# Reordering the end of a quantised stage, weighting rows earlier, and cutting two loads into paced pieces

## The chip, the cores and the metric

The kernel runs on one core of a Trainium2 chip. The metric is the time of one execution in device microseconds (us), lower is better. The engines are PE (matmul), PEld (its weight loads), DVE (vector), ACT (scalar), POOL (GpSimd) and SP (which here issues DMAs only). Each runs its own instruction list in order, and semaphores tie the lists together.

## The reference, cut to what matters

```
x = x + tanh(g_xattn[0]) * state_space(ctx, layernorm(x))
x = x + tanh(g_ffn[0])   * quantised_ffn(layernorm(x))      # 256 -> 1024 -> 256, rows rounded to 8 bits
x = x + tanh(g_xattn[1]) * attention_16_heads(layernorm(x), ctx)
x = x + tanh(g_ffn[1])   * moe_16_experts_top4(layernorm(x)) + shared, sigmoid gate
x = x + tanh(g_xattn[2]) * map_2(layernorm(x), ctx)          # softmax(Q K^T) of ctx alone, applied to x
x = x + tanh(g_ffn[2])   * ffn_with_hadamard(layernorm(x))
x = x + tanh(g_xattn[3]) * map_3(layernorm(x), ctx)
x = x + tanh(g_ffn[3])   * moe_8_experts_top2(layernorm(x)) + shared
```

x is 4 x 256 tokens by 256 columns, ctx is 4 x 256 by 128. In the quantised stage each row of the hidden product is scaled by its largest magnitude / 127, rounded, clipped and multiplied by the down matrix. A routed stage is `silu(x Wg) * (x Wu)`, times the token's weight for the expert, times `Wd`, summed over experts.

## The kernel before, in words

The 1024 tokens lie in 8 tiles of 128 rows and in two halves of 4 tiles. x stays in SBUF. Four parts follow one another: `M` (state space), `F0` (quantised stage), `A1` (attention) and `F` (three feed-forward stages, with the two maps beside them). All f32 products but those of F0 are made of three fp32r matmuls (`mm3`, lines L418 to L420) from a high and a low part of each operand; ACT copies the high part (L852) and DVE or POOL subtracts the low one.

**F0** goes by tiles t = 0 to 7. PE: `gate_up(t)` (L529), `down(t - 3)` (L541), the transposes of the rounded hidden rows `hidden_T(t - 2)` (L554); ACT: Silu (L1023), rounding (L1049), copy of the transposed rows; DVE: product (L1495), the row's largest magnitude (L1498 to L1501), `within_8_bits` (L1483), `output` (L1475). Beside it the inputs of the second half are normalised and quantised (`stats`, `row_scales`, `quantise_x`, `quantised`), and near its end the first four key units of the attention are made in four banks (`key_unit`; their squares by ACT L1042, sums by DVE L1531 `first_key_norms`, roots by POOL L1860) and the first half's rows are normalised (`stats(0)`, POOL's root L1828, `normalise(0)` L1287) and transposed (L413). The last tile's steps are handed to A1 as closures.

**A1** makes 32 passes i (16 heads by two halves). A pass is: queries and the next keys, scores (12 matmuls), their maximum (DVE L1652), Exp (ACT L1180), the row sum's reciprocal (DVE L1684), the weighting of the probabilities by it (POOL L1931), transposes (L732), products with the context and with the folded value-output matrix. POOL's list of a pass is norms, parts of the weights, query norms, then that weighting. The second half's rows must be normalised (`stats(1)`, `normalise(1)`), transposed and split (`x_lo(2)`, L1307) before pass 16.

**F** makes 100 steps g, each one tile of 128 hidden columns for 512 tokens: steps 0 to 55 are the first stage (28 by two halves), 56 to 71 the second, 72 to 99 the third (14 by two halves, of which all but the first two of each half are routed). PE's list at g: `gate_up(g)` (12 matmuls of 512 columns), `side(2g)`, `down(g - 2)` (12 of 256 columns), `side(2g + 1)`. `gate_up(g)` waits for `f_h_lo` of g - 2, since the product is kept in the PSUM bank of its gate. The order on ACT at g: high part of g - 1, Silu of g, side work, issue of DMAs for the routing rows of g + 2, weight parts. DVE's list at g before the change: `weighted(g - 1)` (L1779), `rows_lo(g - 1)` (L1786), `silu_up(g)` (L1579), then side work. `side` runs what the table `beside` puts at a place: normalising, routing, and the maps, which pass through PSUM bank 7 in one fixed order. The first map item is at place 12, so in step 6; it waits for the map weights (`loaded(pe, "am3k")`, L786). The mixing of the second stage's down matrix (L1760, L1768 to L1770) lies at places 22 to 75.

The routing rows of a step (`f_cw`, one expert's weights broadcast over the partitions) come by DMA from ACT's queue (L1082). All weight loads come from SP's queue in the order of `LOADS`; those of step 3 start when A1 has ended:

```python
("f1b", f1b, 3, "f1b"), ("am2q", ...), ("am2k", ...), ("f2w", f2w, 3, "f2"), ("am3q", ...), ("am3k", ...)
```

Of the kernel before, what the change touches and what calls it, by code (L numbers as in the profile page):

```python
# [14 lines left out]
def flamingo_kernel(nc, dram, out):  # L15
# [155 lines left out]
    ktok = [place("B1a", f"a_k_tok{i}", [P, TH, 4, P]) for i in range(2)]  # L171
    ctkh = place("B1a", "a_ctx_tok_hi", [P, NT, P], f32r)
    PTl = place("B1a", "a_PT_lo", [P, 2, HALF], f32r)
    voh, vol = ([place("B1a", f"a_wvo_{n}{i}", [P, DM], f32r) for i in range(2)] for n in ("hi", "lo"))
# [45 lines left out]
    def S(name):  # L220
        if name not in sems:
# [14 lines left out]
        ("f1b", f1b, 3, "f1b"), ("am2q", aw[0], 3, "map"), ("am2k", aw[1], 3, "map"), ("f2w", f2w, 3, "f2"),  # L236
        ("am3q", aw[2], 3, "map"), ("am3k", aw[3], 3, "map"),
# [3 lines left out]
                  for name, _, step, group in LOADS}  # L241

# [91 lines left out]
    put_norm(3, 1, P4 + 17, P4 + 19, P4 + 20, P4 + 22, P4 + 23, P4 + 24, P4 + 26, P5, P5 + 1)  # L334
# [35 lines left out]
    def _(sp):  # L370
        reached = 0

# [5 lines left out]
        for name, dst, step, group in LOADS:  # L378
            if step > reached:
# [13 lines left out]
                reached = step  # L393
            full = tuple(slice(None) for _ in dst.shape)
# [10 lines left out]
    def _(pe):  # L405
# [108 lines left out]
        def ffn0(k, m_output):  # L514
# [44 lines left out]
            for t in range(NT + 2):  # L559
                if t == 3:  # L560
                    pe.wait_ge(S("m_res"), 2)
                    quantised_inputs(1)
                if t < NT:
                    gate_up(t)
# [65 lines left out]
        def attn1(k, ffn0_rest):  # L630
# [50 lines left out]

            keys_queries(0)
            last_hidden_T()
            keys_T(0)
            query_sums(0)
            last_down()
            for i in range(HEADS2 + 2):
                if i + 1 < HEADS2:
                    keys_queries(i + 1)
                if i >= 2:  # L690
# [10 lines left out]
                if i == 1:  # L701
                    pe.wait_ge(S("q_out"), NT)
                    transpose_norm(1, ("A1", 1), (0, 1))
                if i < HEADS2:
                    pe.wait_ge(S("a_kT"), i + 1)
                    pe.wait_ge(S("a_ql"), i + 1)
                    if i:
                        pe.wait_ge(S("a_exp"), i)
                    for t in range(TH):
                        sl = slice(t * P, (t + 1) * P)  # L710
                        kv = slice((t // 2) * DM, (t // 2 + 1) * DM)
                        last = mm3(ps[:, 2 + t // 2, (t % 2) * DM:(t % 2 + 1) * DM], qh[i % 2][:, sl], ql[i % 2][:, sl],
                                   kh[:, kv], kl[:, kv], True, True)
# [1342 lines left out]
```

## Time and profile before

| | us |
|---|---|
| median of 3 runs | 1051.15 (1043.31 to 1052.46) |
| the profiled execution | 1049.61 |
| its span, first to last instruction | 1047.2 |
| PE busy | 922.8 (88%) |
| DVE busy | 728.0 (70%) |
| ACT busy | 643.8 (61%) |
| POOL busy | 484.4 (46%) |

The mean granted clock of TensorE is 0.944 of full speed. By the span's own time, F0 goes from about 180 to 235 us, A1 from there to about 540, F from there to the end. A share of the span is an average over these stages; what an engine does in one stretch is read from the stretch's own rows.

### The profile page before, as it was taken

Reading aid. Unit: us, or ns where it says so; the run is one execution under the profiler, and the core shown is the slowest. Engines: PE = TensorE matmul, PEld = TensorE weight load, DVE = VectorE, ACT = ScalarE, POOL = GpSimd, SP = SyncE. Lnnn points to the kernel's source line nnn. Section 1 sums busy time; section 2 is a strip of 40 time slices with the busy share of each in tenths; the row PEclk is TensorE's granted clock in tenths of the full one; section 3 lists DMA queues with packets and bytes.
Section 4 is the critical chain, followed back from the end, with each engine's and each line's share of the span. In section 5 each row is a group of like instructions: output and inputs, shape, how many; then the busy total and the mean of one; then the engine's idle time right before and its main releaser. Section 6 shows DMA issues by size and latency. Waiting matters only on the chain.

```text
span 1047.2 us, 15667 instructions
## 1 busy us (share of the span) xinstructions
PE 922.8 (88%) x5322; PEld 755.6 (72%) x5322; DVE 728.0 (70%) x1301; ACT 643.8 (61%) x1251; POOL 484.4 (46%) x480
## 2 busy tenths in 40 slices
PE   5277677568999999999887999889999999999998
PEld 1033233247899999999876787777888888888887
DVE  6799998885677767776654466777666565567544
ACT  5857764664777777777554565654667645454553
POOL 0266562143666666666442334345344544344342
PEclk8589989687999999999999899999999999999999
DMA  9200100003000000000039111111111410021121
GB/s 315 117 0 1 60 1 0 1 0 153 1 1 2 2 1 2 1 2 2 1 118 364 44 60 52 41 61 51 49 53 58 156 81 1 1 72 51 51 64 48
DMA packets 16602, 55.97 MB, mean 53 GB/s; under 512 B 2961, under 2 KB 4089, under 8 KB 15149
## 3 DMA queue, kind: packets, MB, share of 16 engines
q1 hardware_dynamic: 4333, 34.01, 8.5%
q10 hardware_dynamic: 12192, 20.98, 6.5%
q8 instruction: 43, 0.70, 0.3%
q14 instruction: 34, 0.28, 0.1%
HBM read 53.82 MB, written 1.16 MB: 52 GB/s over the span
## 4 chain that ended last, share of the span: by engine, by line
PE 44%; DVE 16%; issue 8%; POOL 7%; DMA 4%; ACT 3%; ACTq 1%; SPq 0%; DVEq 0%; POOLq 0%
PE psum L418 12%; PE psum L420 12%; PE psum L419 12%; POOL a_P L1931 3%; DMA am_wk<-in_am3k 3%; DVE a_max L1652 2%; POOL a_rk L1860 2%; DVE psum L1579 2%; POOL a_rq L1868 2%; DVE psum L1779 2%; PE psum L806 1%; PE psum L732 1%; PE psum L670 1%; ACTq L1082 1%; ACT f_h_hi L852 1%
## 5 line engine op out<-in xcount | busy, mean ns | idle before, releaser
L418 PE MATMUL psum<-x_norm_T_hi,f_wgu_hi 128*128 128x512 f32 x400 | 161.8, 405 | 13.8 <-DVE f_h_lo L1786 12.9
L420 PE MATMUL psum<-x_norm_T_hi,f_wgu_lo 128*128 128x512 f32 x400 | 157.9, 395 | 0.0
L419 PE MATMUL psum<-x_norm_T_lo,f_wgu_hi 128*128 128x512 f32 x400 | 157.2, 393 | 0.0
L418 PE MATMUL psum<-f_wd_hi,f_h_hi 128*128 128x256 f32 x400 | 122.7, 307 | 0.1
L1786 DVE TENSOR_TENSOR f_h_lo<-psum,f_h_hi 128x512 fp32r<-128x512 f32 x100 | 69.1, 691 | 75.7 <-ACT f_h_hi L852 75.7
L852 ACT ACTIVATE f_h_hi<-psum 128x512 fp32r<-128x512 f32 x100 | 59.2, 592 | 98.8 <-DVE psum L1779 98.5
L419 PE MATMUL psum<-f_wd_lo,f_h_hi 128*128 128x256 f32 x400 | 113.4, 284 | 0.0
L420 PE MATMUL psum<-f_wd_hi,f_h_lo 128*128 128x256 f32 x400 | 113.4, 283 | 0.0
L1579 DVE TENSOR_TENSOR psum<-f_silu,psum 128x512 f32<-128x512 f32 x100 | 69.2, 692 | 60.2 <-PE psum L420 36.6
L1952 POOL TENSOR_TENSOR m_dBu<-m_du,m_Bs 128x1024 f32<-128x1024 f32 x32 | 76.2, 2381 | 67.7 <-DVE m_du L1377 24.8
L1873 POOL TENSOR_TENSOR f_wgu_lo<-f_w,f_wgu_hi 128x512 fp32r<-128x512 f32 x44 | 56.8, 1291 | 97.3 <-ACT f_wgu_hi L852 97.3
L418 PEld LDWEIGHTS psum<-x_norm_T_hi,f_wgu_hi 128*128 128x128 f32 x400 | 76.1, 190 | 29.7 <-issue 15.3
L1873 POOL TENSOR_TENSOR f_wgu_lo<-f_wb,f_wgu_hi 128x512 fp32r<-128x512 f32 x36 | 46.6, 1295 | 106.2 <-ACT f_wgu_hi L852 106.2
L1931 POOL TENSOR_TENSOR a_P<-a_P,a_row_inv 128x1024 f32<-128x1024 f32 x32 | 60.6, 1894 | 68.6 <-DVE a_row_inv L1684 68.6
L420 PEld LDWEIGHTS psum<-x_norm_T_hi,f_wgu_lo 128*128 128x128 f32 x400 | 75.3, 188 | 17.4
L419 PEld LDWEIGHTS psum<-x_norm_T_lo,f_wgu_hi 128*128 128x128 f32 x400 | 76.2, 190 | 13.3
L419 PEld LDWEIGHTS psum<-f_wd_lo,f_h_hi 128*128 128x128 f32 x400 | 76.8, 192 | 5.0 <-issue 2.2
L418 PEld LDWEIGHTS psum<-f_wd_hi,f_h_hi 128*128 128x128 f32 x400 | 76.6, 191 | 5.2 <-issue 2.5
L420 PEld LDWEIGHTS psum<-f_wd_hi,f_h_lo 128*128 128x128 f32 x400 | 76.8, 192 | 0.0
L1088 ACT ACTIVATE f_silu<-psum 128x512 f32<-128x512 f32 x100 | 59.6, 596 | 26.1 <-PE psum L420 25.8
L852 ACT ACTIVATE a_PT_hi<-psum 128x1024 fp32r<-128x1024 f32 x32 | 32.8, 1025 | 62.9 <-PE psum L732 62.9
L1180 ACT ACTIVATE a_P<-psum,a_neg_max,a_rq 128x256 f32<-128x256 f32 x128 | 70.6, 574 | 0.8 <-DVE a_neg_max L1656 0.8
(316 smaller groups left out, 2654.7 us busy)
## 6 DMA issues: line engine op xcount, KB each, us to landing
f_cw<-r_rows ACTq DMA_DIRECT2D x38, 256.0 KB, 3.1
f_wb<-in_f1b SPq DMA_DIRECT2D x1, 6912.0 KB, 22.0
f_w<-in_f3w SPq DMA_DIRECT2D x1, 5376.0 KB, 16.7
f_wa<-in_f1a SPq DMA_DIRECT2D x1, 3840.0 KB, 11.8
w_raw<-in_w0raw SPq DMA_DIRECT2D x1, 3072.0 KB, 17.9
f_w<-in_f2w SPq DMA_DIRECT2D x1, 3072.0 KB, 31.1
f_cw<-r_rows ACTq DMA_DIRECT2D x12, 224.0 KB, 3.0
f_cw<-r_rows ACTq DMA_DIRECT2D x12, 192.0 KB, 2.8
```

What stands on the lines that cost most here:

```text
L418: mm(out, wh, xh, start=start, stop=False, **kw)
L419: mm(out, wh, xl, start=False, stop=False, **kw)
L420: return mm(out, wl, xh, start=False, stop=stop, **kw)
L852: return A(out_, in_, ACT.Copy)
L1088: A(sg[g % 2][:, :], ps[:, 2 + 2 * (g % 2), :], ACT.Silu).then_inc(S("f_sg"), 1)
L1180: last = A(Pm[i % 2][:, t, :], ps[:, 2 + t // 2, (t % 2) * DM:(t % 2 + 1) * DM], ACT.Exp, bias=nb[:, t:t + 1], scale=rq[i % 2][:, t:t + 1] ...
L1579: V.tensor_tensor(ps[:, 2 + 2 * (g % 2), :], sg[g % 2][:, :], ps[:, 3 + 2 * (g % 2), :], ALU.mult).then_inc(S("f_m"), 1)
L1652: link(V.tensor_reduce(mx[:, :], ps[:, 2:4, :].rearrange("p a (b n) -> p (a b) n", b=2), AX, ALU.max))
L1786: V.tensor_tensor(hl[g % 2][:, :], ps[:, 2 + 2 * (g % 2), :], hh[g % 2][:, :].bitcast(f32), ALU.subtract).then_inc(S("f_hl"), 1)
L1873: G.tensor_tensor(wgl[g % 2][:, :], raw_w(l, j)[:, 0:GU], wgh[g % 2][:, :].bitcast(f32), ALU.subtract).then_inc(S("f_wg"), 1)
L1931: G.tensor_tensor(Pm[i % 2][:, :, :], Pm[i % 2][:, :, :], bc(ri[:, :].unsqueeze(2), [P, TH, DM]), ALU.mult).then_inc(S("a_pn"), 1)
L1952: G.tensor_tensor(dBu[g % 2][:, :, :], du[g // NS][:, :, :], bc(Bs[g % 3][:, :].unsqueeze(1), [P, 2, HALF]), ALU.mult).then_inc(S("m_dBu"), 1)
```

## The change

**Loads.** The four map weights (64 KB each) go ahead of `f1b` (6912 KB) and `f2w` (3072 KB). These two are cut into 6 and 2 pieces, and piece n is issued when `silu_up` has been done n times (`f_m`).

**F0.** PE makes `gate_up(3)` ahead of the second half's input transposes. DVE makes the product ahead of `row_scales(1)`, and `within_8_bits` ahead of `quantise_x` and `quantised`. At t = 7 DVE makes the product, then `stats(0)`, `within_8_bits(6)`, `output(4)`, `normalise(0)`, `first_key_norms`, and only then the last tile's magnitude. The context's high and low parts are made at the end of F0. The last rounding, clipping, transposes and down product move into A1.

**A1.** The first scores come ahead of the last tile's transposes. `output(7)` and `stats(1)` come at the end of DVE's pass 0, and POOL's root for them behind the query norms of pass 0; `normalise(1)` moves from pass 0 to 1, the transposes and `x_lo(2)` from pass 1 to 2, behind the scores of the pass. A one-element Exp is put on ACT ahead of the first pass.

**F.** `weighted(g)` comes right behind `silu_up(g)`, ahead of the side work. For the last half of the third stage, the routing and its top values come half a step to one step earlier.

Buffers of A1 are placed in another order; that hunk and the ones that only rename closures are left out of the diff.

```diff
@@ -233,12 +235,15 @@
...
         ("f1r", fr[1], 2, "route"), ("f1a", f1a, 2, "f1a"),
-        ("f1b", f1b, 3, "f1b"), ("am2q", aw[0], 3, "map"), ("am2k", aw[1], 3, "map"), ("f2w", f2w, 3, "f2"),
-        ("am3q", aw[2], 3, "map"), ("am3k", aw[3], 3, "map"),
+        ("am2q", aw[0], 3, "map"), ("am2k", aw[1], 3, "map"), ("am3q", aw[2], 3, "map"), ("am3k", aw[3], 3, "map"),
+        ("f1b", f1b, 3, "f1b"), ("f2w", f2w, 3, "f2"),
         ("f3r", fr[3], 4, "route"), ("f3w", f3w, 4, "f3"),
...
                   for name, _, step, group in LOADS}
+    PIECES = {"f1b": 6, "f2w": 2}
+    for name, pieces_of in PIECES.items():
+        load_count[name] = (load_count[name][0], 16 * pieces_of)
...
@@ -331,7 +336,7 @@
...
     put_attention(3, 1, P4 + 2, P4 + 5, P4 + 7, P4 + 9, P4 + 11, P4 + 13, P4 + 15)
-    put_norm(3, 1, P4 + 17, P4 + 19, P4 + 20, P4 + 22, P4 + 23, P4 + 24, P4 + 26, P5, P5 + 1)
+    put_norm(3, 1, P4 + 17, P4 + 19, P4 + 20, P4 + 22, P4 + 23, P4 + 24, P4 + 25, P4 + 27, P5 + 1)
     put(P5 + 3, "residual", 3, 0)
...
@@ -369,6 +374,7 @@
...
         reached = 0
+        paced = 0
...
@@ -391,6 +397,13 @@
...
                 reached = step
+            if name in PIECES:
+                n = -(-dst.shape[1] // PIECES[name])
+                for a in range(0, dst.shape[1], n):
+                    paced += 1
+                    sp.wait_ge(S("f_m"), paced)
+                    sp.dma_start(dst[:, a:a + n, :], dram[name][:, a:a + n, :]).then_inc(S("ld_" + group), 16)
+                continue
             full = tuple(slice(None) for _ in dst.shape)
...
@@ -557,11 +570,11 @@
...
             for t in range(NT + 2):
+                if t < NT:
+                    gate_up(t)
                 if t == 3:
...
                     quantised_inputs(1)
-                if t < NT:
-                    gate_up(t)
                 if t == 0:
...
@@ -679,14 +692,28 @@
...
+            def scores(i):
+                pe.wait_ge(S("a_kT"), i + 1)
+                pe.wait_ge(S("a_ql"), i + 1)
+                if i:
+                    pe.wait_ge(S("a_exp"), i)
+                for t in range(TH):
+                    sl = slice(t * P, (t + 1) * P)
+                    kv = slice((t // 2) * DM, (t // 2 + 1) * DM)
+                    last = mm3(ps[:, 2 + t // 2, (t % 2) * DM:(t % 2 + 1) * DM], qh[i % 2][:, sl], ql[i % 2][:, sl],
+                               kh[:, kv], kl[:, kv], True, True)
+                last.then_inc(S("a_s"), 1)
             keys_queries(0)
-            last_hidden_T()
             keys_T(0)
             query_sums(0)
-            last_down()
+            scores(0)
             for i in range(HEADS2 + 2):
...
                     keys_queries(i + 1)
+                if i == 0:
+                    last_hidden_T()
                 if i >= 2:
...
@@ -698,20 +725,10 @@
...
                     last.then_inc(S("a_ac"), 1)
-                if i == 1:
-                    pe.wait_ge(S("q_out"), NT)
+                if 0 < i < HEADS2:
+                    scores(i)
+                if i == 2:
                     transpose_norm(1, ("A1", 1), (0, 1))
-                if i < HEADS2:
-                    pe.wait_ge(S("a_kT"), i + 1)
-                    pe.wait_ge(S("a_ql"), i + 1)
-                    if i:
-                        pe.wait_ge(S("a_exp"), i)
-                    for t in range(TH):
-                        sl = slice(t * P, (t + 1) * P)
-                        kv = slice((t // 2) * DM, (t // 2 + 1) * DM)
-                        last = mm3(ps[:, 2 + t // 2, (t % 2) * DM:(t % 2 + 1) * DM], qh[i % 2][:, sl], ql[i % 2][:, sl],
-                                   kh[:, kv], kl[:, kv], True, True)
-                    last.then_inc(S("a_s"), 1)
                 if i == HEADS2 - 2:
...
@@ -734,6 +751,8 @@
...
                     keys_T(i + 1)
+                if i == 0:
+                    last_down()
                 if i == 2:
...
@@ -1005,6 +1024,13 @@
...
+            def rounded_hidden(i):
+                act.wait_ge(S("q_inv"), i + 1)
+                if i >= 2:
+                    act.wait_ge(S("q_hq"), i - 1)
+                A(h0a[i % 2][:, :], h0[i % 2][:, :], ACT.Identity, scale=qt[i % 2][:, 2:3], bias=magic[:, :]).then_inc(S("q_r"), 1)
             def hidden_copied(t):
...
@@ -1041,17 +1067,16 @@
...
                     last.then_inc(S("a_ksq"), 1)
-                if 1 <= t <= NT:
-                    i = t - 1
-                    act.wait_ge(S("q_inv"), i + 1)
-                    if i >= 2:
-                        act.wait_ge(S("q_hq"), i - 1)
-                    A(h0a[i % 2][:, :], h0[i % 2][:, :], ACT.Identity, scale=qt[i % 2][:, 2:3], bias=magic[:, :]).then_inc(S("q_r"), 1)
+                if 1 <= t < NT:
+                    rounded_hidden(t - 1)
                 if t == 1:
...
                     hidden_copied(t - 2)
-            return lambda: hidden_copied(NT - 1)
+            loaded(act, "ctk")
+            act.wait_ge(S("q_hq"), NT - 1)
+            copy(ctkh[:, :, :], ctk[:, :, :]).then_inc(S("a_ctkh"), 1)
+            return (lambda: rounded_hidden(NT - 1)), (lambda: hidden_copied(NT - 1))
...
@@ -1133,14 +1158,17 @@
...
+            last_hidden_round, last_hidden_copy = last_hidden
             norm_T(1, (6, 5), xTh)
-            copy(ctkh[:, :, :], ctk[:, :, :]).then_inc(S("a_ctkh"), 1)
+            last_hidden_round()
             squares(0)
-            last_hidden_copy()
             keys_hi(0)
+            A(scratch[:, 21:22], epsc[:, :], ACT.Exp)
             for i in range(HEADS2 + 1):
...
                     squares(i + 1)
+                if i == 0:
+                    last_hidden_copy()
                 if i >= 2:
...
@@ -1155,7 +1183,7 @@
...
                     silu(0)
-                if i == 1:
+                if i == 2:
                     norm_T(2, (0, 1), xTa[0])
...
@@ -1486,14 +1514,21 @@
...
                     dve.wait_ge(S("q_r"), t - 1)
-                if t == 1:
-                    row_scales(1)
                 for n in range(2):
...
                                            sg0[t % 2][:, sl], ALU.mult, ALU.mult).then_inc(S("q_h"), 1)
+                if t == 1:
+                    row_scales(1)
+                if t == NT - 1:
+                    dve.wait_ge(S("q_out"), TH)
+                    stats(0)
+                    within_8_bits(NT - 2)
+                    output(NT - 4)
+                    normalise(0, xn[0])
+                    first_key_norms()
                 dve.wait_ge(S("q_h"), 2 * t + 2)
...
@@ -1505,24 +1540,16 @@
...
                     stats(1)
+                if 0 < t < NT - 1:
+                    within_8_bits(t - 1)
                 if t == 1:
...
                     quantised(1)
-                if t == NT - 1:
-                    normalise(0, xn[0])
-                if t:
-                    within_8_bits(t - 1)
-                if t >= 3:
+                if 3 <= t < NT - 1:
                     output(t - 3)
-                if t == NT - 2:
-                    dve.wait_ge(S("q_out"), TH)
-                    stats(0)
             output(NT - 3)
-            first_key_norms()
-            within_8_bits(NT - 1)
-            output(NT - 2)
-            return lambda: output(NT - 1)
+            return (lambda: within_8_bits(NT - 1)), (lambda: output(NT - 2)), (lambda: output(NT - 1))
...
@@ -1627,9 +1654,8 @@
...
             query_norms(0)
-            last_output()
-            dve.wait_ge(S("q_out"), NT)
-            stats(1)
+            for step in last_outputs[:2]:
+                step()
             for i in range(HEADS2):
...
@@ -1645,7 +1671,7 @@
...
                     V.tensor_tensor(xTl[:, c, :], ps[:, 7, :], xTh[:, c, :].bitcast(f32), ALU.subtract).then_inc(S("b7_free"), 1)
-                if i == 1:
+                if i == 2:
                     x_lo(2, (0, 1), xTa[0], xTa[1])
...
@@ -1665,6 +1691,10 @@
...
                 if i == 0:
+                    last_outputs[2]()
+                    dve.wait_ge(S("q_out"), NT)
+                    stats(1)
+                if i == 1:
                     normalise(1, xn[1])
...
@@ -1787,11 +1817,11 @@
...
                 if g:
-                    if WEIGHTED[g - 1]:
-                        weighted(g - 1)
                     rows_lo(g - 1)
...
                     silu_up(g)
+                if g < FN and WEIGHTED[g]:
+                    weighted(g)
                 if g == 1:
...
@@ -1906,12 +1936,11 @@
...
                 norms(0)
+                pool.wait_ge(S("a_ctkh"), 1)
+                G.tensor_tensor(ctkl[:, :, :], ctk[:, :, :], ctkh[:, :, :].bitcast(f32), ALU.subtract).then_inc(S("a_ctk"), 1)
                 continue
             if s == "A1":
-                pool.wait_ge(S("a_ctkh"), 1)
-                G.tensor_tensor(ctkl[:, :, :], ctk[:, :, :], ctkh[:, :, :].bitcast(f32), ALU.subtract).then_inc(S("a_ctk"), 1)
                 norm_q(0)
-                rstd_of()
                 for i in range(HEADS2 + 1):
...
@@ -1921,6 +1950,8 @@
...
                         norm_q(i + 1)
+                    if i == 0:
+                        rstd_of()
                     if i == HEADS + 5:
...
                         rstd_of()
```

## Rows read from the trace of the kernel before

**Rows 1.** Busy time by stretch, PE: stretch, length, busy (count), clock, DMA share, GB/s.

```profile
541.99:581.73 39.74, 30.14 (x154) 0.88 0.81 301
568.77:581.73 12.96, 8.82 (x26) 0.63 0.55 211
220.00:240.00 20.00, 12.30 (x58) 0.68 0.00 1
240.00:260.00 20.00, 18.13 (x91) 0.73 0.50 199
660.00:692.00 32.00, 25.92 (x147) 1.00 0.15 50
692.00:720.00 28.00, 26.22 (x146) 1.00 0.18 59
720.00:760.00 40.00, 39.81 (x219) 1.00 0.17 50
```

**Rows 2.** Who PE waited for, whole span: total us, times, longest.

```profile
PE psum L418 <- DVE f_h_lo L1786: 12.9, 11, 2.8
...
PE psum L529 <- DVE q_h L1495: 5.4, 1, 5.4
...
PE psum L786 <- DMA am_wk<-in_am3k: 4.1, 1, 4.1
...
PE psum L627 <- DVE r_weights L1574: 1.8, 1, 1.8
```

**Rows 3.** Chain of work that ended last, 540 to 580: start, us, what.

```profile
546.62 30.57 DMA am_wk<-in_am3k
```

**Rows 4.** DMA issues from 530 to 600: count, KB each, median us to landing.

```profile
f_wb<-in_f1b SPq DMA_DIRECT2D x1, 6912.0 KB, 22.0
...
f_cw<-r_rows ACTq DMA_DIRECT2D x2, 224.0 KB, 16.9
f_cw<-r_rows ACTq DMA_DIRECT2D x2, 192.0 KB, 3.2
```

**Rows 5.** Instructions in time order, DVE, first steps of F: start, us.

```profile
566.57 0.70 DVE L1779 TENSOR_TENSOR psum<-psum,f_cw 128x512 f32<-128x512 f32 x1 [4.12 <-DMA f_cw<-r_rows]
```

**Rows 6.** The same, PE: first map item and start of `gate_up(7)`.

```profile
577.32 2.05 PE L786 MATMUL psum<-ctx_T,am_wq 128*128 128x512 f32 x2 [4.14 <-DMA am_wk<-in_am3k]
...
581.73 0.56 PE L418 MATMUL psum<-x_norm_T_hi,f_wgu_hi 128*128 128x512 f32 x1
```

**Rows 7.** The same, DVE, end of F0 and passes 0 and 2 of A1.

```profile
219.24 1.41 DVE L1265 BATCH_NORM_STATS2 bn_st<-x_res 128x6 f32<-128x256 f32 x4
...
221.20 1.41 DVE L1495 SCALAR_TENSOR_TENSOR q_h<-psum,q_scales,q_sg 128x512 f32<-128x512 f32 x2
...
250.74 1.22 DVE L1652 TENSOR_REDUCE a_max<-psum 128x4 f32<-128x1024 f32 x1
...
270.33 1.22 DVE L1652 TENSOR_REDUCE a_max<-psum 128x4 f32<-128x1024 f32 x1
```

**Rows 8.** The same, ACT: squares of the key units, table load of pass 0.

```profile
223.66 2.06 ACT L1042 ACTIVATE a_P<-psum 128x512 f32<-128x512 f32 x4 [2.17 <-PE psum L420]
...
252.68 1.28 ACT L1180 ACT_TABLE_LOAD   x1
```

**Rows 9.** The same, POOL: second half's root, first weighting of probabilities.

```profile
246.20 1.01 POOL L1828 TENSOR_TENSOR rstd<-var_eps,minus_half 128x4 f32<-128x4 f32 x1 [2.82 <-DVE var_eps L1279]
...
256.56 1.89 POOL L1931 TENSOR_TENSOR a_P<-a_P,a_row_inv 128x1024 f32<-128x1024 f32 x1 [2.95 <-DVE a_row_inv L1684]
```

**Rows 10.** The same, PE: first query product of A1.

```profile
235.08 0.76 PE L418 MATMUL psum<-x_norm_T_hi,a_w_hi 128*128 128x512 f32 x1 [1.98 <-DVE x_norm_T_lo L1307]
```

**Rows 11.** The same, DVE, end of one step with mixing as side work.

```profile
675.25 1.46 DVE L1768 TENSOR_TENSOR w_mix<-f_w 128x256 f32<-128x256 f32 x1
...
677.95 0.70 DVE L1779 TENSOR_TENSOR psum<-psum,f_cw 128x512 f32<-128x512 f32 x1
679.31 0.69 DVE L1786 TENSOR_TENSOR f_h_lo<-psum,f_h_hi 128x512 fp32r<-128x512 f32 x1 [0.66 <-ACT f_h_hi L852]
```

More of the change, by code:

```diff
@@ L171, in flamingo_kernel @@
     ktok = [place("B1a", f"a_k_tok{i}", [P, TH, 4, P]) for i in range(2)]
+    PTl = place("B1a", "a_PT_lo", [P, 2, HALF], f32r)
+    voh = [place("B1a", f"a_wvo_hi{i}", [P, DM], f32r) for i in range(2)]
+    at["B1a"] += 768
     ctkh = place("B1a", "a_ctx_tok_hi", [P, NT, P], f32r)
-    PTl = place("B1a", "a_PT_lo", [P, 2, HALF], f32r)
-    voh, vol = ([place("B1a", f"a_wvo_{n}{i}", [P, DM], f32r) for i in range(2)] for n in ("hi", "lo"))
+    vol = [place("B1a", f"a_wvo_lo{i}", [P, DM], f32r) for i in range(2)]
     at["B1r"] = at["B1a"]
@@ L1097, in router_exp, with attn1 @@
             A(rp[:, :, 0:e], rw[:, :, 0:e], ACT.Exp).then_inc(S("f_ex"), 1)
-        def attn1(k, last_hidden_copy):
+        def attn1(k, last_hidden):
             def value_parts(i):
@@ L1246, in _ @@
             if s == "A1":
-                attn1(k, last_hidden_copy)
+                attn1(k, last_hidden)
             elif s == "M":
@@ L1252, in _ @@
             else:
-                last_hidden_copy = ffn0(k)
+                last_hidden = ffn0(k)
     @block.vector
@@ L1579, in silu_up, with attn1 @@
             V.tensor_tensor(ps[:, 2 + 2 * (g % 2), :], sg[g % 2][:, :], ps[:, 3 + 2 * (g % 2), :], ALU.mult).then_inc(S("f_m"), 1)
-        def attn1(k, last_output):
+        def attn1(k, last_outputs):
             x_lo(1, (6, 5), xTh, xTl)
@@ L1809, in _ @@
             if s == "A1":
-                attn1(k, last_output)
+                attn1(k, last_outputs)
             elif s == "M":
@@ L1815, in _ @@
             else:
-                last_output = ffn0(k)
+                last_outputs = ffn0(k)
     @block.gpsimd
```

## The prediction

> **What bounds the kernel now.** I read the busy time by stretch first: PE is full in A1 and in most of F (39.81 of 40 us from 720 to 760), with holes in three places: 220 to 260, 541 to 582, and 660 to 720, where it is busy 25.92 of 32 and 26.22 of 28 us [rows 1]. In the first two the granted clock is also down (0.68, 0.73, 0.88). PE's waits name the cause of each hole [rows 2]. Then the chain: from 546.62 one DMA holds it for 30.57 us [rows 3]. In A1's passes the chain turns through DVE's maximum, Exp, POOL's weighting and the next norms; the distance between maxima is 8.5 us a pass, and the change leaves that loop as it is. So the sum has one term for each hole.
>
> **Term 1, the start of F: -10.5 us.** In step 6 PE comes to the first map item and stands for 4.14 us until 577.32 for the last map weight, 64 KB that lie on SP's queue behind 9.9 MB [rows 3, 4, 6]. Before that, DVE stood 4.12 us for a routing row (566.57) issued 14 to 20 us earlier beside the big load; the like takes 3.2 us elsewhere [rows 4, 5], and `gate_up(6)` waited 2.8 us on it [rows 2]. With four small loads ahead (some 1.8 us of issue, 3 us to landing) the map weights are in by about 550, and step 6 needs them near 568. The first pieces of `f1b` go out at 546.3: three in a row, as `silu_up` has then been done twice and is done a third time at 547.7. 6912 KB in 22.0 us make 3.7 us a piece, so SP's load runs until about 557 and then in gaps. The routing rows of step 5 go out near 548.5; with even 14.5 us they land at 563, and `weighted(5)` wants them at 564.7. Those of step 4 now go out at 543.3, ahead of the load. What PE must do from `gate_up(2)` (541.99) to `gate_up(7)` (581.73) is 30.14 us busy; in the last 12.96 us the clock is 0.63, so 9.6 us ran at 1.2 GHz, 4.1 of them idle, and the 5.5 busy ones would take half at 2.4 GHz. That leaves 27.4 us [rows 1, 6]. Waits that stay: 0.7 us before `gate_up(3)` (`rows_lo(1)` behind residual and statistics), 0.3 and 1.0 us at the two transposes of the normalised rows. 27.4 + 2 = 29.4 against 39.74, so 10.3; I take 10.5. Bounds: 12.3 without any wait, and 8 if one routing row is late by 2.5 us.
>
> **Term 2, weighting ahead of the side work: -6.5 us.** The 12.9 us that PE waited for `f_h_lo` are 4.9 in the steps above and 8.1 later, nearly all from 660 to 720, where the side work is the mixing [rows 1, 2]. There DVE goes: `silu_up`, 2.7 us of mixing (675.25 to 677.95), `weighted` 0.70, a wait of 0.66 for ACT's high part, `f_h_lo` 0.69 [rows 11]. With `weighted` first, ACT's part runs beside the mixing, so f_h_lo comes 0.7 us earlier, and one step's DVE work (0.69 x 3 + 2.7 = 4.8 us) is below the 5.7 us in which PE has other products to make (one `gate_up` of 2.8, two `down` of 1.44). Not all steps gain so much: Silu sits behind a table load of 1.28 us in some. I take 6.5 of 8.1; bounds 0 (the wait goes to bank 7's hand-overs, now 0.7 us behind in the list) and 8.1. What else stands behind `weighted` on DVE is the side work; the wait for ACT that stood ahead of it is gone from most steps, so it starts at about the same time.
>
> **Term 3, routing places: -1.3 us.** PE waits 1.8 us for the last routing weights [rows 2]; one step earlier these are ready, which I take whole. Against it, in the first routed step of the third stage (74) the routing rows are issued in the same step: DVE now waits for the landing (3.2 us less the 0.7 of the product) where it did statistics before. Its `f_h_lo` is later by 0.8 us; PE had no wait there, so I take 0.5. Bounds 0 to -1.8, and +1.5.
>
> **Term 4, end of F0 and entry of A1: -6.5 us.** The walk, each step from the durations in the trace:
> - Tile 3 starts earlier. PE waited 5.4 us for the product [rows 2]; `row_scales`, itself waiting 1.1 us for POOL, no longer stands ahead of the product, and `gate_up(3)` no longer behind the inputs' transposes. From tile 3 on DVE is the bound at about 4.3 us a tile, so what holds is the shift of tile 3: 3.5 us.
> - Tile 7's product started at 221.20, behind statistics from 219.24 [rows 7]; now it comes ahead of them, at 215.5. The last key unit is done at 219.9, ACT's squares (2.06 us [rows 8]) at 222.0, the hidden copy at 223.0, the transposes (1.97) at 225.0, DVE's rows and key sums at 224.6, magnitude and one output at 226.9, `x_lo` at 228.1. First query product: 228.2 against 235.08 [rows 10], 6.9 earlier.
> - Pass 0's maximum by the same walk: 244.3 against 250.74 [rows 7]. The Exp table is loaded earlier (1.28 us at 252.68 [rows 8]), so Exp ends 8 us earlier. But `output(7)` and `stats(1)` (2.0 us with the aggregates) now come ahead of the reciprocal, and on POOL the root (1.01) ahead of the weighting [rows 9]; before they lay in idle time. They take 2.1 us back: the weighting starts at 250.3 against 256.56, 6.2 earlier.
> - `x_lo(2)` and its transposes, 1.3 us of DVE behind the scores of pass 2, delay that maximum to 264.8 against 270.33 [rows 7], 5.5 earlier; one more pass gives 6.1. The last tile's rest has its cover in passes 0 and 1; without it, its 1.3 us of ACT and 1.1 of DVE would stand on the path.
> I take 6.5, since PE at the granted clock of 0.7 here [rows 1] may get more. Bounds: 3 (only the statistics behind the product and the table load) and 11 (half of the 9 us that 30.4 busy us lose to the clock given back too).
>
> On the table load the row shows a cost of 1.28 us and nothing idle at either side of it. The Trainium skill (ScalarE: Activation LUTs, What ACT_TABLE_LOAD costs) adds a drain and gives about 2.66 us a switch. By that the sum would be 1.4 us lower; this trace shows no such drain, and the sum goes by 1.28.
>
> **Sum.** 10.5 + 6.5 + 1.3 + 6.5 = 24.8 us off the profiled execution's 1049.6 us: 1024.8. The median shown is 1.5 us above that execution; I add 1: **1026 us**. Ends: 8 + 0 - 1.5 + 3 = 9.5 off gives 1041; 12.3 + 8.1 + 1.8 + 11 = 33.2 off gives 1017.
>
> **The rivals.**
> (a) The routing rows gate DVE. `weighted` wants them one step sooner, and pacing does not pace at first, as three pieces go out together. If those issued at 548.5 and 553 take the 19.6 us of the worst one (the median of two is 16.9 [rows 4]), they land at 568.1 and 572.6 against 564.7 and 570: 3.4 us lost once, since the second wait is within the first. Time 1029 to 1030. For: ranges above. Against: the load has gaps from 557.
> The Trainium skill (DMA: Bandwidth & Descriptors, Queues, rings and completion order) says that each DMA engine takes turns, packet by packet, between queues with work. By that rule cutting a load shortens nothing while a piece is in flight, and only the gaps help. The rows agree so far that a broadcast beside the load took 16.9 us and not the whole 22.0; it leaves rival (a) at this chance and its 3.4 us.
> (b) The mixing stretch gives nothing and the entry is given back inside A1: term 2 at 0 and term 4 at 3, 10.5 + 1.3 + 3 = 14.8 off, 1036. For: PE, DVE and ACT are close there, and hand-built orders shift waits. Against: the wait for ACT's part is plainly behind the side work.
> (c) Slower. `weighted` (0.70 us) ahead of the side work delays bank 7's release, and PE, which takes map, mixing and transposing items in order, stands 0.7 us at each. Some 56 such steps are 39 us; terms 1, 3 and 4 give 18 back: 1070. It decides from about 26 such stops on, and is over 1% slower from some 40. Against: from 720 to 760 PE passes such items in every step and is idle 0.19 us in all [rows 1]; an item has a full step of about 5 us.
>
> **Numbers.** A measurement tells about 1% from no change. Forecast 0.72, (a) 0.11, (b) 0.13, (c) 0.04. Range 1015 to 1041. Faster by over 1% (below 1040.6) 0.90: forecast, (a) and most of (b); within 1% 0.07; slower 0.03.
>
> **What would show it.** Right: PE's wait for `am3k` gone and `gate_up(7)` 29 to 30 us behind `gate_up(2)`; PE busy over 30 of 32 us where the mixing lies; first query product near 228, pass 2's maximum near 265; passes still 8.5 us apart. Wrong: DVE waiting for `f_cw` (a); PE waiting for bank 7's items (c); POOL's first weighting no earlier than 254 (b).

## The result, and the profile after

| us | before | after |
|---|---|---|
| median, runs of the comparison | 1051.8 (4 runs, 1043.3 to 1052.9) | 1021.65 (4 runs, 1020.9 to 1022.3) |
| profiled execution, its span | 1049.6, 1047.2 | 1021.8, 1019.2 |
| PE busy | 922.8 (88%) | 913.8 (90%) |
| mean granted clock | 0.944 | 0.954 |

The ratio is 0.973, with an interval from 0.968 to 0.978. The time lies in the range (1015 to 1041), 4.3 us below the forecast. Three of before's four runs lay high: in the 49 runs of it made beside the experiments, on three chips, the medians were 1046.5, 1046.9 and 1046.2 and the runs went from 1041.7 to 1052.9. Against these the change is worth some 25 us.

**Where the 28.0 us between the two spans came from.** The span is cut at eight marks, read from the time lists: POOL's root for the second half in F0, pass 3's and pass 30's maximum in A1, and `silu_up` (`su`) of steps 0, 8, 56, 74 and 99. The first column of numbers is the time up to the first mark, each other one the distance from the mark before.

```
run              root   ..pass 3  ..pass 30  ..su 0  ..su 8  ..su 56  ..su 74  ..su 99
before          186.59   92.93     230.67     22.70   57.49   240.10    91.33   115.88
after           185.24   87.77     230.72     24.11   45.13   231.29    91.35   114.05
before - after    1.35    5.16      -0.05     -1.41   12.36     8.81    -0.02     1.83
```

Busy time by stretch of the changed kernel (stretch, length, PE busy and count, PEld, DVE, ACT, POOL, granted clock, DMA share, GB/s). The first runs from `gate_up(2)` to 0.1 us behind the start of `gate_up(7)` (564.49), as the first of [rows 1]; the last three lie over the mixing:

```profile
536.85:564.60 27.75, 26.31 (x155) 22.52 (x156) 20.50 (x54) 15.02 (x28) 11.28 (x12) 1.00 0.90 314
220.00:240.00 20.00, 14.06 (x54) 11.41 (x55) 13.21 (x21) 7.84 (x11) 9.22 (x7) 0.66 0.00 1
240.00:260.00 20.00, 16.06 (x90) 13.24 (x89) 13.30 (x31) 12.63 (x32) 9.77 (x13) 0.83 0.50 199
640.00:672.00 32.00, 30.83 (x176) 26.57 (x175) 23.53 (x46) 21.54 (x39) 15.29 (x15) 1.00 0.23 66
672.00:700.00 28.00, 27.83 (x157) 23.94 (x156) 24.02 (x43) 14.82 (x28) 14.42 (x15) 1.00 0.17 58
700.00:740.00 40.00, 40.00 (x227) 34.88 (x226) 25.37 (x52) 27.00 (x46) 14.51 (x15) 1.00 0.15 47
```

39.74 us at a clock of 0.88 became 27.75 at 1.00, and the mixing stretch is full. The hole at 220 to 260 is still there, and the clock is still down (0.66 and 0.83, against 0.68 and 0.73). PE's waits over the whole span, the counterpart of [rows 2]:

```profile
PE psum L542 <- DVE q_h L1521: 4.7, 2, 4.0
...
PE psum L426 <- DVE x_norm L1315: 4.0, 1, 4.0
...
PE psum L431 <- DVE f_h_lo L1816: 2.5, 5, 0.8
...
PE psum L431 <- POOL f_wgu_lo L1903: 2.2, 2, 2.1
```

The wait for `am3k` and that for the last routing weights are gone, and 12.9 us for `f_h_lo` are 2.5. New are 4.0 us for the normalised rows. The wait for a weight's low part has grown from 0.7 to 2.2, and those inside the attention for `a_qT_lo` and `a_AC_lo` from 1.7 and 1.9 to 3.9 and 3.1.

### The profile page after: what moved, and what is told of

Its sections match the earlier page's. It is cut to its first block, busy times and chain, and to the rows that moved or that the text cites. A ratio compares the mean times of both kernels' runs of the same rounds, so it can differ in the third digit from the quotient of the medians.

```text
span 1019.2 us, 15670 instructions
## 1 busy us (share of the span) xinstructions
PE 913.8 (90%) x5319; PEld 752.0 (74%) x5322; DVE 723.6 (71%) x1301; ACT 645.7 (63%) x1252; POOL 484.5 (48%) x480
## 4 chain that ended last, share of the span: by engine, by line
PE 51%; DVE 13%; POOL 8%; issue 7%; ACT 2%; ACTq 1%; DMA 1%; DVEq 0%; POOLq 0%
PE psum L431 14%; PE psum L433 14%; PE psum L432 14%; POOL a_P L1962 3%; DVE a_max L1678 2%; POOL a_rk L1890 2%; POOL a_rq L1898 2%; DVE psum L1606 1%; PE psum L825 1%; PE psum L749 1%; DVE psum L1809 1%; PE psum L683 1%; DVE bn_st L1293 1%; DVE x_norm L1315 1%; PE psum L785 1%
## 5 line engine op out<-in xcount | busy, mean ns | idle before, releaser
L1983 POOL TENSOR_TENSOR m_dBu<-m_du,m_Bs 128x1024 f32<-128x1024 f32 x32 | 76.2, 2382 | 66.2 <-DVE m_du L1405 24.8
L1113 ACT ACTIVATE f_silu<-psum 128x512 f32<-128x512 f32 x100 | 59.7, 597 | 39.9 <-PE psum L433 39.7
```

Source lines behind the costliest of these rows:

```text
L1113: A(sg[g % 2][:, :], ps[:, 2 + 2 * (g % 2), :], ACT.Silu).then_inc(S("f_sg"), 1)
L1983: G.tensor_tensor(dBu[g % 2][:, :, :], du[g // NS][:, :, :], bc(Bs[g % 3][:, :].unsqueeze(1), [P, 2, HALF]), ALU.mult).then_inc(S("m_dBu"), 1)
```

## The experiments

Twelve kernels, each in five rounds against the kernel before on its chip (e on one chip, a on a second, c on a third). Distances to the changed kernel are between medians, its own from the comparison above; before's medians on the three chips differ by 0.7 us. The changed kernel itself was not run again on these chips, so a distance of 2 to 3 us to it is surer in the traces' marks than in the medians: as ratios to before, a3 (0.973) and a4 (0.972) lie inside the changed kernel's interval.

**e1_order: the order of the loads alone.**

```diff
-  ("f1b", ...), ("am2q", ...), ("am2k", ...), ("f2w", ...), ("am3q", ...), ("am3k", ...),
+  ("am2q", ...), ("am2k", ...), ("am3q", ...), ("am3k", ...), ("f1b", ...), ("f2w", ...),
```

> The kernel before with the four map weights ahead of the two big loads, which stay whole; nothing else. Theory (each half of the load change has its own share): PE's wait of 4.1 us for the last map weight goes and the clock comes back sooner, but the routing rows of step 5 still land 14 to 20 us after their issue, beside a load of 6912 KB, and DVE still stands some 4 us for them; so the distance from gate_up(2) to gate_up(7) falls from 39.7 to 33 to 35 us and the kernel gets 5 to 7 us faster. Rival (the order alone was the cause): distance 28 to 29 us as in the changed kernel, 11 to 12 us faster.

Measured: 1046.31 us, ratio 1.000 (0.998 to 1.003). Both expectations were wrong: no gain at all. PE's waits and DVE's product with the routing rows, 530 to 600:

```profile
PE psum L418 <- DVE f_h_lo L1786: 8.8, 4, 5.8
```

```profile
L1779 DVE TENSOR_TENSOR psum<-psum,f_cw 128x512 f32<-128x512 f32 x11 | 7.6, 694 | 10.4 <-DMA f_cw<-r_rows 10.4
```

The map weights came in 2 us, PE's 4.1 us for them went, and DVE's wait for routing rows grew from 4.4 to 10.4 us. DVE stood 7.1 us for the rows of step 4, on whose product `gate_up(6)` waited 5.8 us, and 3.1 us more for those of step 5. All these rows were issued beside the load. DMA issues in that window:

```profile
f_wb<-in_f1b SPq DMA_DIRECT2D x1, 6912.0 KB, 21.6
...
f_cw<-r_rows ACTq DMA_DIRECT2D x2, 224.0 KB, 21.0
...
f_cw<-r_rows ACTq DMA_DIRECT2D x2, 128.0 KB, 23.9
```

So there were two stalls, the rows' and the map weights', and with the second gone the first took as long as both had.

**e2_order_paced: the order and the pieces.**

```diff
+    PIECES = {"f1b": 6, "f2w": 2}
...
+                    sp.wait_ge(S("f_m"), paced)
+                    sp.dma_start(dst[:, a:a + n, :], ...)
```

> As the last, and the two loads in 6 and 2 pieces, each issued after one more silu_up. Theory: as the start of F in the changed kernel: gate_up(2) to gate_up(7) in 28 to 29 us, no wait of DVE for routing rows, 11 to 12 us faster than before. Rival (in the changed kernel part of the gain here came from the early weighting): distance 31 us or more, 7 to 9 us faster.

Measured: 1034.31 us, ratio 0.990 (0.987 to 0.993), so 10.4 us (by the medians 12.2). From `silu_up(0)` to `silu_up(8)` it took 47.04 us against 57.49: **10.45 us** less, where the prediction's term 1 has 10.5. From `gate_up(2)` to `gate_up(7)`, the term's own marks, it took 28.8 against 39.7 us, as the theory said. DVE's wait for the rows (530 to 600) fell to 0.4 us. In the changed kernel the stretch of eight steps takes 45.13; the other 1.9 us are the early weighting's.

The pieces did not open gaps in the load. In the changed kernel some piece was in flight from 541.5 to 577.9 us, as each was issued before the last had landed, and the DMA engines were no less busy than beside the whole load (columns as above; the changed kernel, then e1):

```profile
544.00:564.00 20.00, 19.34 (x119) 16.58 (x118) 12.93 (x30) 11.43 (x20) 6.44 (x7) 1.00 1.01 376
```

```profile
544.00:564.00 20.00, 16.72 (x104) 14.39 (x104) 8.64 (x17) 5.34 (x12) 6.03 (x6) 1.00 0.93 380
```

What differed is how much was in flight beside a row: one to four pieces of 1152 KB, each 5.7 to 12.2 us to landing, and not 9984 KB at once. Whether the cutting or the later issue does it is not shown: no run has pieces without the waits, or the whole load issued later.

**e3_weighting: the early weighting alone.**

```diff
                 if g:
-                    if WEIGHTED[g - 1]:
-                        weighted(g - 1)
                     rows_lo(g - 1)
                 if 0 < g < FN:
                     silu_up(g)
+                if g < FN and WEIGHTED[g]:
+                    weighted(g)
```

> The kernel before with weighted(g) right behind silu_up(g), ahead of the side work; loads whole and in the old order. Theory: PE waits 8 to 9 us less for the rows' low part in steps 17 to 40, and since PE still stands for the last map weight at 577 us, the start of F changes by under 1.5 us: 7 to 10 us faster in all. Rival (routing rows gate DVE): rows issued beside the whole load land 14 to 20 us later and are now wanted one step sooner, so DVE stands 4 to 8 us longer for them in steps 4 to 6 and gate_up(7) begins 2 to 5 us later than at 581.7: 3 to 6 us faster in all.

Measured: 1035.56 us, ratio 0.989 (0.986 to 0.993), 11 us. Steps 8 to 56 took 231.28 us against 240.10 (8.8 less), steps 0 to 8 took 57.97 (0.5 more): PE came sooner to the first map item (563.7 us for 573.2) and there stood 10.3 us for `am3k` instead of 4.1. Third stage: 0.95 less. That is 9.3 us by the marks, inside the theory's 7 to 10. Of the 9.5 us at the map item 4.2 had come ahead of F, where the instructions are before's. The rival did not show: DVE stood 5.2 us for rows, 4.4 in before.

**a1_unpaced and a2_late_weighting: one part taken out of the changed kernel.** a2 is e3's diff backwards; a1:

```diff
-    PIECES = {"f1b": 6, "f2w": 2}
+    PIECES = {}
```

> The changed kernel with the two big loads whole again (map weights still ahead). Theory (pieces let the routing rows through; with the early weighting these are wanted one step sooner): rows issued beside the load land 14 to 24 us later, DVE stands 10 to 16 us for them in steps 3 to 6, and the kernel takes 1033 to 1037 us, 11 to 15 over the changed one. Rival (with the map weights ahead the load's size matters little once weighting is early): 1023 to 1027 us.

Measured: 1031.02 us (1029.7 to 1033.2), 9.4 above the changed kernel, between the two expectations. By the marks nearly all of it, 8.15 us, is in steps 0 to 8 (53.28 us for 45.13), where PE stood once for 5.3 us, and DVE 11.0 us in all for rows:

```profile
L1809 DVE TENSOR_TENSOR psum<-psum,f_cw 128x512 f32<-128x512 f32 x12 | 8.4, 700 | 11.3 <-DMA f_cw<-r_rows 11.0
```

> The changed kernel with weighted(g - 1) back behind the side work. Theory (the parts add up): the start of F as in the changed kernel within 1 us, PE stands 8 to 9 us more for f_h_lo in the mixing steps, 1031 to 1033 us. Rival (with PE full at the start of F each late step costs more than the kernel before showed): 1035 us or more.

Measured: 1034.66 us (1030.6 to 1036.9), 13.0 above, between the two expectations. By the marks the parts add up: 46.90, 240.12 and 116.04 us in steps 0 to 8, 8 to 56 and 74 to 99, against 45.13, 231.29 and 114.05, together 12.6.

**e4_entry: the new end of F0 and entry of A1 alone**, all hunks on the four engines but the early weighting, and the buffers. Its core on DVE:

```diff
+                if t == NT - 1:
+                    dve.wait_ge(S("q_out"), TH)
+                    stats(0)
...
+                    normalise(0, xn[0])
+                    first_key_norms()
```

**c1_old_entry** is its mirror: the changed kernel with those hunks undone.

> The kernel before with the new order at the end of the quantised stage and in the entry of the attention alone; the loads and the third part as before. Theory: the passes of the attention run 5 us earlier (passes 3 to 30) and the third part starts 4 to 5 us earlier; 4 to 5 us faster. Rival (the walk of the prediction, with the granted clock as its upside): 6 to 7 us or more. Second rival (the 1.3 us by which the state-space part ran earlier in the changed kernel come from the new placing of buffers): that part ends 1.3 us earlier here too.

Measured: 1045.65 us, ratio 0.999 (0.997 to 1.001): no gain that can be told. Root to pass 3 took 87.76 us, 5.2 less than in the first trace. But steps 8 to 56, whose code is before's, took 242.28 us against 240.10, and 1.5 of these 2.2 us are in step 27, where the clock fell once behind a wait of 1.98 us (0.82 and 0.84 from 685 to 695). The placing of buffers is out as a cause of the 1.35 us ahead of the root: here the root came at 186.64.

> The changed kernel with the old order at the end of the quantised stage and in the attention's entry; its load change and early weighting stay. Theory (the entry's 5.1 us in the two traces are in part the old entry's luck: from the end of the state-space stage to pass 3's maximum the old order took 0, 3.0, 3.0 and 6.6 us less than in the first trace, the new one 5.1 to 5.9): 1022 to 1025 us, 1 to 3 over the changed kernel, and a spread of 5 us or more where that has 1.4. Rival (the new entry is worth its 5.1 us): 1026 to 1028 us.

Measured: 1027.71 us (1023.2 to 1029.9, 6 runs), 6.1 above the changed kernel. Here the rival held by its size, and the theory by the spread. The two runs disagree on what the entry is worth, and the profiled executions show two reasons. One lies outside the entry: c1's steps 8 to 56 took 232.94 us and not 231.29, with the clock at 0.66 from 755 to 760 behind the wait of 2.06 us for POOL's part, a wait that the changed kernel has too without such a fall. So in these traces 1.65 us of c1's distance and 2.2 us that e4 lost are not the entry's. The other is the entry's own spread. The distance from root to pass 3, all runs with neither filling nor moved root:

```
old order:  92.93 (before)  89.91 (e1)  86.29 (e2)  89.92 (e3)  92.97 (c1)   mean 90.4
new order:  87.76 (e4)      87.77 (after)  87.00 (a1)  87.04 (a2)            mean 87.4
```

The same instructions in the same order took 86.3 to 93.0 us. The granted clock makes the difference. From 215 us to pass 3's maximum its mean was 0.79 in before and c1, 0.83 in e1 and e3, 0.91 in e2; that is 27, 20.5 and 10 us at half the clock, in the order of the distances. In the four of the new order it was 0.82 to 0.83, again 20.5 us: at the same time at half the clock the new order took 2.1 to 2.9 us less than the old. Before, and then e2 (columns as above):

```profile
230.00:235.00 5.00, 3.10 (x15) 2.19 (x13) 2.72 (x6) 2.03 (x3) 4.56 (x3) 0.50 0.00 0
235.00:240.00 5.00, 4.66 (x19) 3.41 (x19) 2.91 (x5) 1.98 (x4) 1.24 (x1) 0.50 0.01 3
240.00:245.00 5.00, 5.00 (x20) 4.22 (x21) 2.30 (x6) 0.59 (x2) 1.20 (x2) 0.50 0.00 0
```

```profile
230.00:235.00 5.00, 3.13 (x15) 2.19 (x13) 2.72 (x6) 2.03 (x3) 4.54 (x3) 0.63 0.00 0
235.00:240.00 5.00, 4.02 (x30) 3.18 (x31) 3.54 (x6) 2.58 (x4) 1.28 (x1) 1.00 0.01 3
240.00:245.00 5.00, 4.16 (x27) 3.51 (x25) 3.94 (x14) 1.87 (x4) 2.80 (x5) 1.00 0.62 197
```

Up to 233 us they are alike: PE idle for 3.7 us until 227.3, the clock down to 0.5 at 227. Then it came back at 233.7 in e2 and at 247.6 in before. In 13.9 us at half the clock a busy PE does 7 us less work than at full; the two distances differ by 6.6. (Later falls, 3.4 us once in e2 and twice in before, blur this sum.) Over before's 27 runs beside e1 to e4 the span followed the mean clock: 1040.1 us for the three at 0.953 and 0.954, 1047.9 us for the two at 0.944.

**c2_old_entry_filled, a4_filled, c3_new_filled: is it the clock?** Transposes of a constant fill PE's waits and touch nothing that is read; where a bank must first be free, a wait for it goes ahead of them. From a4:

```diff
+        def fill(n, bank):
+            for _ in range(n):
+                nc.tensor.transpose(ps[:, bank, 0:P], ident[:, :], ident[:, :])
...
+                    fill(12, 6)
                     pe.wait_ge(S("q_hT"), NT - 1)
                     transpose_norm(0, ("A1", 0), (6, 5))
```

> As the last, with 36 transposes of a constant added on PE in the waits of the old entry (14, 4, 7, 4, 4, 3), into banks that nobody reads. Theory (the old entry's spread is the time at which the granted clock comes back): the clock is at 1.0 for most of 227 to 250 us, the spread falls under 3 us and the median by 3 to 5 us against the same kernel unfilled: 1018 to 1021 us. Rival (the spread has another source): spread and median as without, or 1 to 3 us slower by the added work.

Measured: 1021.50 us (1019.9 to 1023.1). Against c1, on the same chip, that is 6.2 us less, more than expected, and the spread is 3.2 us for 6.7. Root to pass 3: 86.77 us. From 240 to 250, where c1 has 0.50 and 0.73:

```profile
240.00:245.00 5.00, 5.00 (x37) 4.47 (x36) 3.95 (x14) 1.64 (x4) 2.30 (x4) 1.00 0.42 105
245.00:250.00 5.00, 3.74 (x24) 3.02 (x23) 4.36 (x9) 2.56 (x4) 3.11 (x5) 1.00 1.08 462
```

> The changed kernel with 32 transposes of a constant added on PE (12, 7, 3, 7, 3) into banks that nobody reads, in the five waits between the last key unit and pass 2; nothing else. Theory (what the entry of the attention costs is the granted clock that falls after each wait and comes back after 4 to 10 us of work): with the waits filled the clock stays at 1.0 from 216 to 256 us, pass 3's maximum comes 3 to 6 us earlier, and the kernel takes 1016 to 1019 us with a spread as small as before. Rival (DVE and ACT set the pace there, and PE has room at half the clock): pass 3's maximum moves by under 1 us either way. Second rival (the clock falls all the same): the filling adds up to 3 us.

Measured: 1018.65 us (1016.6 to 1019.3), 3.0 below the changed kernel; root to pass 3 took 85.10 us. The clock was at 1.00 from 238 to 251, not all the way: a 2.7 us wait ahead of the transposes was left, and it fell at 224, and again at 234, for 3.4 us each.

**a3_root_later: POOL's parts ahead of the root.**

```diff
                 key_weights_lo(2)
-                rstd_of()
                 parts(1)
                 key_weights_lo(3)
                 context_lo(1)
+                rstd_of()
```

> The changed kernel with POOL's last low parts (weights and context) ahead of the root for the first half's statistics: these had been ready for 3 us while POOL stood idle. Theory (the four normalise instructions took 3.69 us instead of 2.17 because POOL worked on SBUF beside them): they take 2.2 us again, the root ends 0.4 us later, the first query product comes 1.1 us earlier and the kernel gains 0 to 1 us, the granted clock permitting. Rival (it is not POOL): they stay at 3.7 us and the kernel loses 0.4 us.

Measured: 1019.13 us (1018.2 to 1021.2), 2.5 below the changed kernel, more than expected; root to pass 3 took 84.14 us. The four normalise instructions (DVE; ns least, median and most of one), the changed kernel's and then a3's:

```profile
L1315 DVE TENSOR_SCALAR x_norm<-x_res,bn_mv,rstd x4: 399/1087/1354, 219.0 to 222.3; 128x256 f32<-128x256 f32 x4
```

```profile
L1315 DVE TENSOR_SCALAR x_norm<-x_res,bn_mv,rstd x4: 405/406/412, 220.1 to 221.1; 128x256 f32<-128x256 f32 x4
```

POOL at the same time in the changed kernel:

```profile
218.90 0.73 POOL L1863 TENSOR_TENSOR a_w_lo<-a_wq,a_w_hi 128x256 fp32r<-128x256 f32 x1
219.59 1.31 POOL L1876 TENSOR_TENSOR a_wk_lo<-a_wk,a_wk_hi 128x512 fp32r<-128x512 f32 x1
220.87 1.31 POOL L1870 TENSOR_TENSOR a_ctxT_lo<-ctx_T,a_ctxT_hi 128x512 fp32r<-128x512 f32 x1
```

e4, a1, a2 and a4, with POOL as here, show 1353 to 1359 ns for the longest; c3, with POOL as in a3, 413. So the cause is POOL: the four took 1.4 us in a3 and 3.7 in the changed kernel, 2.3 us less. The other 1.3 us of root to pass 3 go with the clock (PE's wait fell from 4.0 to 2.3 us, and the clock stayed at 1.00 through the transposes), which was not tested apart.

> The changed kernel with both gains of the last four runs: POOL's low parts ahead of the root, and PE's waits filled (10, 4, 5, 8, 5, 3 transposes of a constant). Theory (the two are separate, 2.5 and 3.0 us, but both work by the clock): 1015.5 to 1018 us. Rival (the first already kept the clock up through the first hole, so the second adds nothing): 1018.5 to 1019.5 us.

Measured: 1014.71 us (1013.8 to 1016.6), ratio to before 0.969 (0.965 to 0.972); root to pass 3 took 81.26 us, the shortest with the next one's (81.44). The two gains add up, and to more than the sum of the medians: 6.9 us below the changed kernel, where a3 and a4 have 2.5 and 3.0. With the root moved, the fillings still gave 4.4 us against a3 (on another chip), so the rival is out.

**c4_filled_root_behind: the new wait of the mixing stretch.** c3, and on POOL in F:

```diff
-                    side(2 * g)
                     if g + 2 < FN:
                         gu_lo(g + 2)
+                    side(2 * g)
```

> As the last, and in F POOL makes gate_up's low weight part ahead of the root for the normalised rows where both fall in one step (PE waited 2.06 us for that part at 745 us). Theory: that wait falls to some 0.8 us and nothing else moves: 1.3 us less than the last. Rival (the rows' normalising then comes late, and PE waits there instead): no gain, or up to 2 us more.

Measured: 1012.83 us (1011.7 to 1014.6), ratio to before 0.966 (0.963 to 0.970). That is 1.9 below c3 on the same chip, a little more than expected, and steps 8 to 56 took 229.21 us against 231.35. This is the fastest version. What had been wrong, in a4's trace (POOL):

```profile
744.61 1.01 POOL L1870 TENSOR_TENSOR rstd<-var_eps,minus_half 128x4 f32<-128x4 f32 x1 [4.16 <-DVE var_eps L1319]
745.59 1.27 POOL L1915 TENSOR_TENSOR f_wgu_lo<-f_wb,f_wgu_hi 128x512 fp32r<-128x512 f32 x1
```

ACT had that part's high half ready at 744.25; POOL stood for statistics and made the root first.

## Why the prediction was right, point by point

- **Term 1 (10.5): right in size.** e2 has 10.45 by its marks. The stated bound of one late row did not come into play: the rows issued at 546.1 and 546.6 landed in 8.2 and 9.6 us, where the walk left 14.5. But two of its reasons were wrong. The prediction gave the first 4.1 us to the map weights, and e1 shows that order alone is worth nothing: the rows' wait grew by 6.0 us. And it had the load run in gaps from about 557, where the trace has pieces in flight until 577.9 and a DMA share of 0.96 from 564 to 574. That the size held is in part the room that the walk had left. The pieces carry the whole term, on condition that the order is there. The old order with pieces was not tried: there `am3k` would lie behind a piece that step 7 releases, and step 7 behind `am3k`.
- **Rival (a), rows gating DVE:** not seen with pieces (0.6 us in all for the product's idle time). Without them it is the main cost, 9.4 us (a1), nearly three times the 3.4 us that the rival named. The prediction said that pacing does not pace at first; the worst median of rows beside the pieces was 8.9 us. The Trainium skill (DMA: Bandwidth & Descriptors, Queues, rings and completion order) has the engines take turns packet by packet. By it rows beside a load need not wait for its end; in e1 they landed 21.0 and 23.9 us after issue beside a load of 21.6. So in e1 they took about as long as the load, and beside pieces (9.2 us, median) at most about as long as a piece. The prediction said that by this rule only gaps would help; there were none, and the rows still came sooner.
- **Term 2 (6.5, bound 8.1): too small.** 8.8 us in steps 8 to 56, 1.9 in steps 0 to 8, and about 1 in the third stage. The waits that it priced did as it said: those named `f_h_lo` in that stretch fell from 8.1 to 1.2 us, 6.9 against 6.5. What failed is that the bound took them for all that the late weighting cost. PE's idle time in steps 8 to 56 fell from 10.6 to 3.9 us, and its busy time by 2.1 (229.46 to 227.41) for the same 1278 matmuls; that this is waiting which stood in the trace as busy time is likely, but not shown. Of 11.3 us gained by step 34, 2.5 were gone by step 56; one wait of 2.06 us for POOL's part, 0.67 before, is among them, and c4 takes it away. **Rival (c)**, bank 7's hand-overs, did not occur: PE is busy 40.00 of 40 us.
- **Term 3 (1.3): near in size (1.8, the end of its bounds), wrong in its cause.** The early weighting alone gives 0.95 (e3). The places alone give nothing (a2): the wait of 1.8 us for the routing weights went, and waits of 1.2 and 0.4 us for `f_h_lo` came. Only together do they give 1.8.
- **Term 4 (6.5): the step that was mis-sized.** The walk's marks were met: tile 3's product 4.8 us earlier, tile 7's at 214.1 (215.5), the first query product at 228.6 (228.2), pass 0's maximum at 243.9 (244.3), POOL's first weighting at 251.1 (250.3), pass 2's maximum at 265.2 (264.8), the passes 8.54 us apart. But 1.35 us of each came from ahead of F0 (tile 3: 3.4 net, 3.5 said). So the marks were met with help from outside the term; net, pass 2's maximum came 3.8 us earlier and not 5.5. What failed is `normalise(0)`, taken at 2.2 us: moved to where POOL makes low parts, it took 3.7. Net 5.2 us in the two traces, of which 1.4 went back at the end of A1: that execution had the clock at 0.62 from 515 to 520, where a3 has 1.00, and all other runs of the new order took 22.0 to 22.9 us there and not 24.1. And the trace of before was a long one here: against the mean of five executions of the old order the new one gains 3.0. Medians give 0.9 (e4) and 6.1 (c1), and both hold falls of the clock in F (2.2 and 1.65 us in the traces). So the new order is worth some 3 us, with 1 to 6 not excluded. Whether it also narrows the spread is not shown: 1.4 us in the changed kernel's 4 runs, but 6.4 in a2 and 7.3 in e4.
- **The +1 for the median:** the profiled execution of before is 3 us above the median of its 49 runs, not 1.5 below it. Three runs could not show that. That the sum (24.8) meets the 25 us against before's usual median is luck: in the traces terms 1 to 3 gave 23.0 us for 18.3, term 4 gave 3.7 (5.2 less the 1.4) for 6.5, 1.35 came from ahead of F0, and the trace of before lay 3 us high. The range's lower end, 1015, is 2 us below what its own terms give (1017); nothing rests on it.
- On the table load, the row after is 1.28 us again, with ACT's next instruction right behind it. The sum by 1.28 stands.

Left open: why the state-space part ended between 185.2 and 188.5 us in executions of the same instructions, in which instructions the 2.1 us of busy time were, and why the clock fell in F behind a wait of 2.06 us in c1 and c2 and not in the others.

## What to carry to other kernels

A stall that the chain of waits names can cover another just as long on a different engine: ask what the next instruction behind it waits for before pricing its removal, and test the parts apart. Bulk loads cut into pieces and tied to progress let small latency-bound transfers through. Where PE stands for a few us, as here for 2 to 4, the clock that is granted afterwards can be a cost of its own with a spread of several us; look at several executions, shorten or fill the waits, and keep POOL's streaming work away from DVE instructions on the critical path.

## What the runs showed of the hardware

- The same instructions of that stretch, with the same 3.7 us of PE idle ahead of them, ran at half the clock for 7 us in one execution and for 20 in another (e2, 227 to 233.7; before, 227 to 247.6). Constant transposes in the waits cut this: c1 to c2, 6.2 us of median and half the spread.
- A DVE TENSOR_SCALAR of 128x256 f32 from SBUF to SBUF took 0.41 us with POOL's f32 subtractions in SBUF moved away (a3, c3) and up to 1.36 beside them.
- A broadcast of 128 to 224 KB beside a load of 6912 KB took 12.6 to 23.9 us to land (medians of pairs in before, e1 and a1), beside pieces of 1152 KB 3.5 to 8.9 (after, e2), and 2.5 to 3.0 over the whole of before (medians of twelve). The DMA engines' share was 1.01 beside the pieces and 0.93 beside the whole load.
